# Attention values' products of eight heads in one piece and one PSUM bank, and three banks in turn for the scores

## What is computed

```python
x = x + tanh(g_xattn[0]) * L0_xattn(layernorm(x), ctx, ctx, mask, W_q, W_k, W_v, W_proj, b)
x = x + tanh(g_ffn[0])   * L0_ffn(layernorm(x), w_gate, w_up, w_down)
x = x + tanh(g_xattn[1]) * L1_xattn(layernorm(x), ctx, ctx, Wq, Wk, Wv, Wo, bo)
x = x + tanh(g_ffn[1])   * L1_moe(layernorm(x), w_router, w_gate, w_up, w_down)
# attention, per head: softmax(q @ k.T / 4 [masked]) @ v, then the output projection
```

## Time and profile before

| | us |
|---|---|
| median of three timed runs | 1279.74 (1276.01 to 1280.07) |
| the profiled execution, own time | 1273.72 |
| its span, first to last instruction | 1272.5 |
| PE busy in the span | 1194.9 |
| DVE busy | 893.5 |
| ACT busy | 709.6 |
| POOL busy | 482.1 |

### The profile page before, as it was taken

How to read it: one execution, slowest core, us unless ns; L and a number is a source line. 1 busy time by engine, 2 the same in 40 slices (tenths; PEclk the granted TensorE clock), 3 DMA queues, 4 the chain that set the end, 5 groups by cost and what they waited for, 6 DMA issues and landing times.

```text
span 1272.5 us, 25177 instructions
## 1 busy us (share of the span) xinstructions
PE 1194.9 (94%) x9260; PEld 857.0 (67%) x9260; DVE 893.5 (70%) x2680; ACT 709.6 (56%) x1197; POOL 482.1 (38%) x677
## 2 busy tenths in 40 slices
PE   7799999999999989999999979999999999988998
PEld 6477677776777654444458866677677677578987
DVE  4677777876787646589999865777877868652333
ACT  2455555555555538899873326666566566622221
POOL 5444334443343000067000434444643643323555
PEclk9999999999999999999999999999999999999999
DMA  6423333233422041000004553445455342148973
GB/s 187 136 81 105 93 96 110 83 112 99 125 86 62 11 141 43 1 1 2 1 1 133 157 167 110 121 137 165 126 160 150 106 138 78 52 151 250 306 195 36
DMA packets 121942, 137.22 MB, mean 108 GB/s; under 512 B 12882, under 2 KB 116428, under 8 KB 121798
## 3 DMA queue, kind: packets, MB, share of 16 engines
q1 hardware_dynamic: 111888, 125.98, 33.4%
q0 software_dynamic: 7296, 8.15, 3.5%
q10 hardware_dynamic: 2634, 1.49, 0.5%
HBM read 58.42 MB, written 27.36 MB: 67 GB/s over the span
## 4 chain that ended last, share of the span: by engine, by line
PE 53%; DVE 7%; issue 4%; ACT 2%; POOL 2%; SPq 1%; DMA 1%; ACTq 0%; POOLq 0%; DVEq 0%
PE PS L669 14%; PE PS L715 6%; PE PS L470 5%; PE PS L410 5%; PE PS L453 4%; PE PS L429 4%; PE PS L683 3%; PE PS L724 2%; PE PS L502 2%; PE PS L528 2%; PE PS L417 2%; DVE NM L1119 1%; PE PS L546 1%; ACT P L839 1%; PE PS L511 1%
## 5 line engine op out<-in xcount | busy, mean ns | idle before, releaser
L839 ACT ACTIVATE P<-PS 128x512 f32<-128x512 f32 x512 | 302.6, 602 | 162.3 <-PE PS L456 88.1
L1116 DVE CUSTOM_DVE_ANT_0 MX<-PS,NQ 128x256 bf16<-128x256 f32 x512 | 192.5, 418 | 67.9 <-PE PS L429 67.8
L453 PE MATMUL PS<-QS,KS 99*128 99x256 bf16 x1024 | 226.3, 274 | 7.8 <-ACT P L839 6.7
L1119 DVE TENSOR_REDUCE NM<-PS 128x2 f32<-128x512 f32 x256 | 173.4, 685 | 71.7 <-PE PS L429 70.5
L429 PE MATMUL PS<-KS,QS 96*128 96x256 bf16 x1024 | 196.5, 274 | 24.0 <-DVE NM L1116 14.5
L429 PEld LDWEIGHTS PS<-KS,QS 96*128 96x128 bf16 x1024 | 86.7, 97 | 89.3 <-DVE NM L1116 27.0
L470 PE MATMUL PS<-P,V 128*32 128x256 f32 x2048 | 138.3, 388 | 1.5 <-ACT P L839 1.5
L453 PEld LDWEIGHTS PS<-QS,KS 99*128 99x128 bf16 x1024 | 96.0, 99 | 50.3 <-ACT P L839 20.5
L456 PE MATMUL PS<-NK,identb 128*128 128x256 bf16 x512 | 127.9, 274 | 0.0
L669 PE MATMUL PS<-XNT,wup 128*128 128x512 f16 x576 | 124.9, 379 | 0.0
L669 PEld LDWEIGHTS PS<-XNT,wup 128*128 128x128 f16 x576 | 56.2, 98 | 67.4
(11 more groups left out here) (234 smaller groups left out, 2466.7 us busy)
## 6 DMA issues: line engine op xcount, KB each, us to landing
KS<-PP SPq DMA_DIRECT2D x192, 128.0 KB, 3.0
QS<-PP SPq DMA_DIRECT2D x192, 128.0 KB, 2.4
WH<-in_wex SPq DMA_DIRECT2D x16, 768.0 KB, 8.0
WG<-in_wex SPq DMA_DIRECT2D x10, 768.0 KB, 5.3
bufd<-bias_row SPq DMA_DIRECT2D x5, 1032.0 KB, 12.4
XB<-in_x SPq DMA_DIRECT2D x16, 256.0 KB, 3.5
CT<-in_ctxT SPq DMA_DIRECT2D x16, 256.0 KB, 3.8
x1d<-XB SPq DMA_DIRECT2D x16, 256.0 KB, 2.1
```

Of the source, the lines that this page charges most:

```text
L453: ins = tensor.matmul(o, t.KS[b % 3][0:99, h, 128 * kt:128 * kt + 128], t.QS[b % 3][0:99, h, :], start=True, stop=(L == 1))
L839: scalar.activation(t.P[h % 8][:, :, :], PS[:, h % 2, :].rearrange("p (k n) -> p k n", k=2), ACT.Exp).then_inc(s_ex, 1)
L1116: ins = vector.tensor_tensor_reduce(t.MX[:, 2 * (h % 2) + qt, :], PS[:, bk, 256 * qt:256 * qt + 256], t.NQ[b % 4][:, qt, :], -1.0, 1.0e30, ...
L1119: ins = vector.tensor_reduce(nm[:, :, h], PS[:, bk, :].rearrange("p (t n) -> p t n", t=2), X, ALU.max, negate=True)
```

## The change

The values' products of eight heads become one piece: slot 9 for heads 0 to 7, slot 1 of the next row for heads 8 to 15. Both use bank 4. ACT's copies move with them, from slot 12 to slot 10 and from slot 3 to slot 2, and OT has one buffer. The ring P grows from eight tiles to ten, indexed by i. Bank 5, now free, joins banks 2 and 3 for the scores: three banks in turn, and `pe_scores` waits for the maxima of head i - 3 (heads 0 to 7 of layer 1's first batch keep their four banks). The tile MX, into which DVE's masked maxima write their by-product, grows to six rows. The filler matmuls go to bank 4, and counts of s_ah, now two per batch, are halved where they are waited for.

```diff
+NP_RING = 10
+def score_turn(L, b, h):
+    return (16 * (L * NB + b) + h) % 3
 def score_bank(L, b, h):
-    return 2 + h % (4 if (L, b) == (1, 0) and h < 8 else 2)
+    if (L, b) == (1, 0) and h < 8:
+        return 2 + h % 4
+    return (2, 3, 5)[score_turn(L, b, h)]
...
-            t.P = [tile(m, f"P{i}", [128, 2, 256], F32) for i in range(8)]
-            t.OT = [tile(m, f"OT{i}", [128, 4, 256], F32) for i in range(2)]
+            t.P = [tile(m, f"P{i}", [128, 2, 256], F32) for i in range(NP_RING)]
+            t.OT = tile(m, "OT", [128, 4, 256], F32)
...
-            pe.wait_ge(s_mx, i - (3 if (L, b) == (1, 0) and h < 8 else 1))
+            pe.wait_ge(s_mx, i - (3 if (L, b) == (1, 0) and h < 8 else 2))
...
-        def pe_av(L, b, g):
-            ob = 4 + g // 2
-            pe.wait_ge(s_ex, 16 * n + 4 * g + 4)
-            if g % 2 == 0:
-                pe.wait_ge(s_ot, 2 * (n - 1) + g // 2 + 1)
-            for kt in range(2):
-                for i in range(4):
-                    h = 4 * g + i
-                    ins = tensor.matmul(PS[32 * i:32 * i + 32, ob, 256 * (g % 2):256 * (g % 2) + 256],
-                                        t.V[b % 3][:, kt, h, :], t.P[h % 8][:, kt, :], start=(kt == 0), stop=(kt == 1))
+        def pe_av(L, b, hh):
+            pe.wait_ge(s_ex, 16 * n + 8 * hh + 8)
+            pe.wait_ge(s_ot, 2 * n + hh)
+            for g in range(2):
+                for kt in range(2):
+                    for i in range(4):
+                        h = 8 * hh + 4 * g + i
+                        ins = tensor.matmul(PS[32 * i:32 * i + 32, 4, 256 * g:256 * g + 256], t.V[b % 3][:, kt, h, :],
+                                            t.P[(16 * n + h) % NP_RING][:, kt, :], start=(kt == 0), stop=(kt == 1))
             ins.then_inc(s_ah, 1)
...
         def pe_slot(L, s, k):
                 pe_scores_t(L, s, k)
-                if k in (5, 9, 13):
-                    pe_av(L, s, (k - 5) // 4)
+                if k == 9:
+                    pe_av(L, s, 0)
...
                 if k == 1:
-                    pe_av(L, s - 1, 3)
+                    pe_av(L, s - 1, 1)
...
         def act_exp(L, b, h):
-            act.wait_ge(s_ah, 4 * n + h // 4 - 1)
+            act.wait_ge(s_ah, (i - NP_RING) // 8 + 1)
             act.wait_ge(s_st, i + 1)
...
         def act_heads(L, b, hh):
-            act.wait_ge(s_otr, 2 * (n - 1))
-            act.wait_ge(s_ah, 4 * n + 2 * hh + 2)
+            act.wait_ge(s_otr, 2 * n)
+            act.wait_ge(s_ah, 2 * n + hh + 1)
...
         def act_slot(L, s, k):
-            if 0 <= s < NB and k == 12:
+            if 0 <= s < NB and k == 10:
                 act_heads(L, s, 0)
...
-                if k == 3:
+                if k == 2:
                     act_heads(L, s - 1, 1)
```

More of the change, by code:

```diff
@@ L241, in late_tiles @@
                 t.NQ = [tile(m, f"NQ{i}", [128, 2, 256], BF16) for i in range(4)]
-                t.MX = tile(m, "MX", [128, 4, 256], BF16)
+                t.MX = tile(m, "MX", [128, 6, 256], BF16)
                 t.NK = [tile(m, f"NK{i}", [128, 2, 256], BF16) for i in range(4)]
@@ L510, in pe_heads @@
             for g in range(4):
-                ins = tensor.transpose(PS[:, bk, 128 * g:128 * g + 128], t.OT[b % 2][:, g, 128 * qt:128 * qt + 128],
+                ins = tensor.transpose(PS[:, bk, 128 * g:128 * g + 128], t.OT[:, g, 128 * qt:128 * qt + 128],
                                        ident[:, :])
@@ L563, in pe_slot @@
                 pe_scores_t(L, s, k)
-                if k in (5, 9, 13):
-                    pe_av(L, s, (k - 5) // 4)
+                if k == 9:
+                    pe_av(L, s, 0)
             if 0 <= s + 1 < NB:
                 if (L, s, k) == (1, -1, 2):
-                    pe_warm(5, 8)
+                    pe_warm(4, 8)
                 for h in scores_at(L, s, k):
@@ L583, in pe_slot @@
                     if (L, b) == (0, 0):
-                        pe_warm(5, 12)
+                        pe_warm(4, 12)
                     pe_values(L, b)
@@ L594, in pe_slot @@
                     if L == 1 and s == NB:
-                        pe_warm(5, 6)
+                        pe_warm(4, 6)
                     pe_out(L, s - 1)
@@ L599, in pe_slot @@
                     if s - 2 == NB - 1:
-                        pe_warm(5, 14)
+                        pe_warm(4, 14)
                     pe_xm(L, s - 2)
@@ L605, in pe_slot @@
                     if s - 2 == NB - 1:
-                        pe_warm(5, 10)
+                        pe_warm(4, 10)
                     pe_ranks(GROUP_OF[s - 2][0])
@@ L752, in pe_program @@
             pe.wait_ge(s_cst, 1)
-            pe_warm(5, 20)
+            pe_warm(4, 20)
             for s, k in slots(0):
                 pe_slot(0, s, k)
-            pe_warm(5, 6)
+            pe_warm(4, 6)
             pe.wait_ge(s_am, NB)
@@ L759, in pe_program @@
             pe_scale_b(0)
-            pe_warm(5, 13)
+            pe_warm(4, 13)
             for i in range(NCH):
@@ L796, in pe_program @@
             pe.wait_ge(s_pos, 6)
-            pe_warm(5, 30)
+            pe_warm(4, 30)
             pe_turn(0)
@@ L836, in act_exp @@
             i = 16 * n + h
-            act.wait_ge(s_ah, 4 * n + h // 4 - 1)
+            act.wait_ge(s_ah, (i - NP_RING) // 8 + 1)
             act.wait_ge(s_st, i + 1)
-            scalar.activation(t.P[h % 8][:, :, :], PS[:, h % 2, :].rearrange("p (k n) -> p k n", k=2),
+            scalar.activation(t.P[i % NP_RING][:, :, :], PS[:, h % 2, :].rearrange("p (k n) -> p k n", k=2),
                               ACT.Exp).then_inc(s_ex, 1)
@@ L843, in act_heads @@
             n, t = L * NB + b, TL[L]
-            act.wait_ge(s_otr, 2 * (n - 1))
-            act.wait_ge(s_ah, 4 * n + 2 * hh + 2)
-            scalar.activation(t.OT[b % 2][:, 2 * hh:2 * hh + 2, :], PS[:, 4 + hh, :].rearrange("p (g n) -> p g n", g=2),
+            act.wait_ge(s_otr, 2 * n)
+            act.wait_ge(s_ah, 2 * n + hh + 1)
+            scalar.activation(t.OT[:, 2 * hh:2 * hh + 2, :], PS[:, 4, :].rearrange("p (g n) -> p g n", g=2),
                               ACT.Copy).then_inc(s_ot, 1)
@@ L882, in act_values @@
             act.wait_ge(s_iv, 3 * L + min(b, 2) + 1)
-            act.wait_ge(s_ah, 4 * (n - 2))
+            act.wait_ge(s_ah, 2 * (n - 2))
             act.wait_ge(s_vp, n + 1)
@@ L1115, in dve_max @@
                 for qt in range(2):
-                    ins = vector.tensor_tensor_reduce(t.MX[:, 2 * (h % 2) + qt, :], PS[:, bk, 256 * qt:256 * qt + 256],
+                    ins = vector.tensor_tensor_reduce(t.MX[:, 2 * score_turn(L, b, h) + qt, :], PS[:, bk, 256 * qt:256 * qt + 256],
                                                       t.NQ[b % 4][:, qt, :], -1.0, 1.0e30, ALU.add, ALU.min, nm[:, qt, h:h + 1])
@@ L1826, in sp_expert_weights @@
                 sp.wait_ge(s_st, 32 * NB)
-                sp.wait_ge(s_ah, 8 * NB)
+                sp.wait_ge(s_ah, 4 * NB)
                 sp.wait_ge(s_otr, 4 * NB)
```

## The result

The changed kernel takes 1266.6 us (median of four runs, 1264.9 to 1271.8) where the kernel before takes 1279.9 (four runs; the three listed ahead gave 1279.7): ratio 0.991, interval 0.989 to 0.994, so 0.9% faster. 27.4 us were forecast, 13.3 came: right in sign, inside the range, and less than half in size. A second set of runs gave 1263.9 against 1276.8, ratio 0.990 (0.987 to 0.994).

The account below looks back on a forecast made before the run. PE was taken to bound both attention stretches, with DVE second. Junctions -15.4, third bank -20, moved pieces +7 and layers' ends +1 sum to -27.4 us, from 1279.7 to 1252.3 us; range 1236 to 1272.

Parts of the forecast that it names:

- Junctions: Joining two four-head pieces on PE removes 64 junctions of 0.24 us, saving 15.4 us; an eight-head piece takes 1.96 us.
- The first rival: Values' products: holes come with each group of four heads, so joining saves nothing; 1267.7 us, chance 0.08.
- the sum: Whole kernel: junctions -15.4, third bank -20, moved pieces +7, layers' ends +1, giving -27.4 us.
- the second rival: Third bank only moves PE's wait to the ON transposes or ACT's copies; 1272.3 us, chance 0.12.
- its sign: Waits on ON or on the exponentials growing by more than 8 us would show the second rival.
- the third bank's term: Score matmuls wait less for DVE's maxima with three banks: 20 us saved over 30 batches, 0.67 us each.
- slot 13's lost cover: The piece missing from slot 13, under which ACT and DVE caught up, was costed at nothing.
- The moved pieces: Slot 5 loses its piece, so PE waits: 5.3 us in layer 1, 1.5 in layer 0, together 7 us.
- The wait of the OT transposes: Layer 1, after slot 5: PE waits for ACT's copies, 0.35 us a batch, 5.3 us over 15 batches.
- The layers' ends: The longer last piece in each layer's closing serial chain costs 1 us, bounds 0 and 1.7.
- The third rival: Cover lost at slots 5 and 13 returns as PE waits, making the kernel slower; 1311 us, chance 0.08.
- The point at which the sign turns: The kernel gets slower once returning waits exceed 1.15 of the 2.20 us a batch at slots 5 and 13.

Follow-up runs that it names:

- e1: Changed kernel with the scores back in two banks in turn, joined pieces kept; 1297.1 us, ratio 1.012 to the kernel before.
- e2: Changed kernel with pieces of four heads again, at slots 5, 9, 13 and 1, third score bank kept; 1270.6 us, ratio 0.992 to the kernel before.
- e4: Changed kernel with the ON transposes and ACT's copy of them moved from slot 8 to slot 9; 1261.9 us, ratio 0.986 to the kernel before.
- e3: Changed kernel with ACT's copy of OT's second half moved from slot 2 to the end of slot 1; 1261.3 us, ratio 0.985 to the kernel before.
- e10: Changed kernel, OT second-half copy in slot 1, values' copy in 14, layer 0's ON transposes and copy in 9, layer 1's first half split at 5 and 9; 1247.4 us.

## Why the prediction was half right

**Junctions: right.** 1.95 us for eight heads, forecast 1.96, twice a batch in both layers. The first rival (holes with every four heads) is out: it would have made the piece 2.20 us, twice the 1.10 of four heads.

**Layer 0: right in sum, by luck in its parts.** Forecast 1.05 us a batch, measured 26.58 to 25.53. But the sum took 0.48 for the junctions and 0.67 for the bank as if they were separate. e1 and e2 say 0.27 and 0.48 alone, 1.05 together. And the second rival was in part true here: the ON transposes' wait rose from 3.9 to 10.3 us, by 6.4 where its sign was 8, and e4 won 0.35 us a batch back by moving them.

**Layer 1: the step that failed is the third bank's term, added up as if it stood alone.** The 5.8 us of waits beyond the pieces in layer 1's stretch were pooled with layer 0's and spread over all batches, and the bank was given 0.67 us in every batch of both layers. Beside pieces of four heads an ordinary batch of layer 1 has nothing of it: 22.66 with three banks, 22.67 with two. The 5.8 us lie beside the routing and in the last batches. A mean over batches of several kinds was put in place of a look at one of each. The cost of this error is 0.67 us a batch, about 9 us over layer 1.

The same four kernels can be read from the other end. Beside joined pieces the third bank is worth 0.70 us in such a batch (e1 23.52, changed 22.82), about what was forecast. But it only pays for the 0.71 us of slot 13's lost cover, which the sum had at nothing. Either way the two were no independent terms, and together they come to nothing where the sum had -0.67.

**The moved pieces: one term near, one not priced.** The wait of the OT transposes was forecast at 0.35 us a batch. The rows have 0.21 at the first and 0.14 at its followers. ACT's order, the reason given, is shown for 0.20 of them by e3; the small waits around the transposes stay in e3 and go only with the piece in slot 5 (e10), so that the total of 0.35 came out is in part luck. The router's wait for DVE grew by 0.26 us and had no term. I had priced slot 5's cover against ACT only, and there is a third engine behind it. 0.26 us in 15 batches are 4 us. With it the layer 1 sum reads -0.48 + 0.35 + 0.26 = 0.13 us; measured 0.15.

**The layers' ends: no cost seen.** The sum had 1 us for the longer last piece. In the second profile, whose ends have the upper clock, the last batches take 12.90 and 12.12 us, before the change 12.96 and 12.19.

**The third rival was nearer than its 8%.** Lost cover is real. Without the third bank it returns 1.33 us a batch in layer 1, far more than the junctions' 0.48, and the kernel is 1.2% slower. With it 0.61 us return, still more than 0.48, and that is why layer 1's ordinary batches became longer. The point at which the sign turns was put at 1.15 us, but that counts a gain of 0.67 from the bank, which layer 1 does not have beside the cover's loss.

**Two baselines.** The profiled execution before the change (1273.7 us) ran at a clock of 0.992, and the span of the profile after is only 6.1 us shorter; the medians differ by 13.3. The forecast was carried to the median, which the batch lengths bear out; a reader who compares the two profiles alone would halve the gain again.

## What to carry to other kernels

Work on the bounding engine that stands between two dependent steps is cover for the other engines. Before moving or joining such pieces, list for each slot that loses one which of all other engines were catching up under it, and look at the buffers that must then hold the lag; a second buffer and a denser schedule are one change, not two. And read waits from one batch of each kind, not from a mean over a stretch: a wait of 5.8 us in nine batches was zero in the ordinary ones. When an overlap is lost, look first at the order of single instructions: two copies moved on ACT, one transpose moved with its copy, and one piece put back were worth more here than the change itself.

## What the runs showed of the hardware

Going from full-width matmuls to a piece of 32 columns and back costs PE 0.24 us (0.09 before, 0.15 behind), for a piece of four heads (1.10 us in all) as for one of eight (1.95 us). The Trainium skill, "TensorEngine Tiling (Array Packing)", Key Properties, says that a change of tiling mode, and not of the tile alone, drains TensorE. The traces agree: no hole came between the two groups of four heads. ACT's copies and exponentials of 512 columns last 0.60 us in the rows but follow each other every 0.48 us. A DMA that ACT itself issues behind its copy keeps ACT from its next instruction for 0.81 us (the idle time in the row of 942.29). It is as long in the kernel before (0.82 us at 951.75) and in e3, where the OT transposes' wait is gone, so it alone did not make that wait. The four runs of the changed kernel took 1264.9 to 1271.8 us at granted clocks of 0.985 to 0.977 over the span. In its first profile stretches at the lower level lie at the ends of both layers (0.79 over 445 to 460 us, 0.83 to 0.85 over 1110 to 1130).
